# State-space stages of a four-layer kernel: decay by one spreading product per unit, difference and rectifier on ScalarE, causal limit as a 0/1 product on VectorE

## The chip, the cores and the metric

The kernel runs on one core of one Trainium2 chip. A core has TensorE (matrix products, written to PSUM), VectorE, ScalarE, GpSimd and SyncE, each with its own queue that it works through in order; they wait for each other through semaphores. The metric is the time of one execution on the device in microseconds (us), the median of several runs.

## The reference, cut to what matters

The whole program is a stack of four layers, each a mixer and a feed-forward part, over 16 sequences of 256 tokens with 128 channels. Two of the mixers are state-space stages, and only these are touched. The recurrence of the third layer's mixer, with 16 heads of width 16 and a state of 64:

```python
delta = softplus(dt + delta_param)
a_bar = exp(-delta * abs(dt))
h = a_t[:, :, None, None] * h + x_t[..., None] * b_t[:, :, None, :]
y_t = einsum('bhds,bhs->bhd', h, c_t)
```

The fourth layer's mixer (called mamba in the kernel) is of the same kind, with 4 heads of width 64, one B and C for all heads, and `A_bar = exp(A * dt)`. In both, the decay between step s and a later step t is the exponential of the difference of two cumulative sums of logarithms, `exp(cum[t] - cum[s])`, for t >= s and zero for t < s, and all logarithms are at most zero.

## The kernel before

`ssm_block` (from line 901) builds both stages; `ssm` is the stage with 16 heads, `mamba` the one with 4. The 16 sequences are worked in 8 pairs, the first written out (`pair(0, False)`) and the others in a hardware loop. A pair has a setup and a loop over units.

In the setup TensorE projects the input (lines 1062 to 1069), ScalarE and VectorE take the results, VectorE convolves, and from line 1396 on VectorE makes the cumulative sum `cum` of the logarithms and splits it into three bf16 parts, which lie one under the other in `parts` (96 rows, lines 1411 to 1418).

A unit is one head of one sequence, so there are 32 units in a pair of `ssm` and 8 in a pair of `mamba`. It works on 384 columns: the 256 query steps against the first 128 key steps, and the last 128 query steps against the last 128 key steps. The steps of unit u are:

- `unit(u)` on TensorE (line 1117). In each of two column groups `pick` times `parts` spreads the query side's sum (line 1128), `parts` times `unpick` subtracts the key side's sum (line 1130), and `ident16` times `future` adds a very negative number where the key is later than the query (line 1132). That fills `dbank[u % 2]` and counts `decay_up`. Then, for `ssm` in every unit and for `mamba` once per sequence, come the scores, C against B (lines 1150 and 1151), which count `scores_up`.
- ScalarE, line 1281: one `Exp` of 384 columns from `dbank` into `decay[u % 2]`, which counts `decay_done`.
- VectorE, line 1465: `decay` times scores gives `mixer[u % 2]`, which counts `mixer_done`. For `ssm` the scores are read from PSUM, for `mamba` from a copy that line 1457 makes once per sequence.
- `mix(u)` on TensorE: the products of `mixer` with the inputs (lines 1164 and 1165 for `ssm`, 1170 to 1172 for `mamba`), which count `y_up`.

TensorE's order is written out by hand. It looks one unit ahead:

```python
unit(0)
for u in range(units):
    if u + 1 < units:
        unit(u + 1)
    ...
    mix(u)
```

ScalarE's order in the loop is wait for `decay_up` of u, wait for `mixer_done` of u - 2, `Exp` of u. Between some units the late work of the pair before is put in: on VectorE the norms of the tail after units 1, 4 and 7 (0, 2 and 4 in `mamba`), on TensorE and ScalarE the transposes of the tail in `ssm` after unit 10 (lines 171 and 176), and after half of the units VectorE's `take_gated` (lines 1348 and 1353).

Of the kernel before, what the change touches and what calls it, by code (L numbers as in the profile page):

```python
# [20 lines left out]
P = 128  # L21
TILES = SEQS * SEQ // P
PAIRS = SEQS // 2
PT = 4
# [876 lines left out]
def ssm_block(core, name, tail, heads, mamba):  # L901
# [26 lines left out]
    with ExitStack() as ctx:  # L928
# [7 lines left out]
        ident16, future = sb("ident16", [P, P], BF16), sb("future", [P, P], BF16)  # L936
# [40 lines left out]
        decay_up, decay_done = sem("decay_up"), sem("decay_done")  # L977
        scores_up, scores_taken = sem("scores_up"), sem("scores_taken")
# [4 lines left out]
        loads = 12  # L983
# [19 lines left out]
        @block.sync  # L1003
        def _(sp):
            for to, what in ((wx, "wx"), (wdt, "wdt"), (wbc, "wbc"), (wgate, "wgate"), (wout, "wout"), (taps, "taps"),
                             (cols, "cols"), (head_cols, "head_cols"), (pick, "pick"), (unpick, "unpick"),):
                sp.dma_start(to[:], dram[f"{name}_{what}"]).then_inc(weights_in, 16)
            sp.dma_start(ident16[:], dram["identity16"]).then_inc(weights_in, 16)
            sp.dma_start(future[:], dram["future"]).then_inc(weights_in, 16)
# [32 lines left out]
        def _(pe):  # L1042
# [71 lines left out]
            def pair(i, has_late):  # L1114
# [3 lines left out]
                def unit(u):  # L1118
# [6 lines left out]
                    if not (isinstance(i, int) and u < 2):  # L1125
                        pe.wait_ge(decay_done, n - 1)
                    for col, rows, width in ((0, s[0], SEQ), (SEQ, s[1], P)):
                        pe.matmul(bank[:, col:col + width], pick[:, h, :], parts[:, rows:rows + width],
                                  start=True, stop=False)
                        pe.matmul(bank[:, col:col + width], parts[:, rows:rows + P],  # L1130
                                  unpick[:, h:h + 1].broadcast_to([96, width]), start=False, stop=False)
                        last = pe.matmul(bank[:, col:col + P], ident16[:], future[:], start=False, stop=True)  # L1132
                    last.then_inc(decay_up, 1)
# [48 lines left out]
                for kind, n in first_items[-3:-1]:  # L1182
                    _, side, before = place(i, kind, n)
                    pe.wait_ge(down[side], before + 1)
                unit(0)
# [17 lines left out]
        def _(act):  # L1203
# [9 lines left out]
            def pair(i, has_late):  # L1213
# [57 lines left out]
                for c in range(CH):  # L1271
                    act.wait_ge(conv_ready, i * CH + c + 1)
                    flat = conv[:, c].rearrange("p j t -> p (j t)")
                    act.activation(flat, flat, ACT.Silu).then_inc(x_bent, 1)
                for u in range(units):
                    n = i * units + u
                    act.wait_ge(decay_up, n + 1)
# [3 lines left out]
                    act.activation(decay[:, u % 2, :], dbank[u % 2][:, 0:SPAN], ACT.Exp).then_inc(decay_done, 1)  # L1281
# [42 lines left out]
        def _(dve):  # L1324
# [43 lines left out]
            def pair(i, has_late):  # L1368
# [80 lines left out]
                for u in range(units):  # L1449
                    j, h = divmod(u, heads)  # L1450
                    n = i * units + u
                    if not mamba:
                        dve.wait_ge(scores_up, n + 1)
                        scored = gbank[u % 2][:, 0:SPAN]
                    elif h == 0:
                        dve.wait_ge(scores_up, i * 2 + j + 1)
                        dve.tensor_copy(scores[:], gbank[0][:, 0:SPAN]).then_inc(scores_taken, 1)
                        dve.drain()
# [7 lines left out]
                    ins.then_inc(mixer_done, 1)  # L1466
                    if not mamba:
                        dve.drain()
                        dve.sem_inc(scores_taken, 1)
                    if u == heads - 1:  # L1470
                        take_gated(i, 0)
# [1841 lines left out]
def arrange(inputs):  # L3313
# [52 lines left out]
    out["future"] = np.where(t[:, None] <= t[None, :], 0.0, -BIG).astype(bf16)  # L3366
# [96 lines left out]
```

## Time and profile before

| what | value |
|---|---|
| median of 3 runs | 5105.25 us (5102.89 to 5107.88) |
| the profiled execution, its own time | 5086.59 us |
| its span, from first to last instruction | 5084.6 us |
| mean granted clock of TensorE over the span | 0.863 of 2.4 GHz |
| busy share: TensorE, VectorE, ScalarE, GpSimd | 77%, 51%, 44%, 21% |
| the unit loops of `ssm`, first to last start of line 1281 | 2725.7 to 3513.0 us |
| the unit loops of `mamba`, the same | 4081.8 to 4447.5 us |

The profile is of one execution. Busy shares are averages over all the stages, which have different limits, so the two stages have to be read by themselves: in the timeline each row has a start, a length, the engine, the line of the kernel and, in brackets, how long the engine was idle before it and what ended that. The two stages take some 790 and 370 us of the span.

### The profile page before, as it was taken

How to read it: one execution, taken by the hardware profiler on the slowest of the kernel's cores; microseconds unless marked ns; L12 is line 12 of the kernel's file. 1: busy time of each engine (PE TensorE's matmuls, PEld its weight loads, DVE VectorE, ACT ScalarE, POOL GpSimd, SP SyncE). 2: the span in 40 equal slices, each digit the busy share in tenths (PEclk: the TensorE clock that was granted, in tenths of full speed). 3: DMA queues.
4: the chain of work that ended last, by engine and by line, in shares of the span. 5: the costliest groups of instructions: out<-in, count | busy, mean ns of one | idle time of the engine just before them, and what ended most of it. 6: DMA issues, size and time to landing. Idle time of an engine off the chain costs nothing. (4 is left out here: it accounts for less than half of the span.)

```text
span 5084.6 us, 65295 instructions
## 1 busy us (share of the span) xinstructions
PE 3893.2 (77%) x19738; PEld 2713.3 (53%) x19800; DVE 2569.9 (51%) x6625; ACT 2231.9 (44%) x4312; POOL 1045.3 (21%) x1066
## 2 busy tenths in 40 slices
PE   3659954999967688878877888987999877720398
PEld 1137722677734455546555667765677555520266
DVE  5858744222234766477864343342222255579544
ACT  3446533333442688778863433342333333300133
POOL 1012211000001666366640000000000000154200
PEclk9879977899976799989998999998999966655599
DMA  1420021000000000000000000000000000000000
GB/s 38 76 51 7 6 75 54 1 0 0 0 20 0 18 1 0 1 18 1 0 1 16 1 0 0 0 0 33 1 0 0 5 1 0 0 1 0 18 0 17
DMA packets 45622, 58.55 MB, mean 12 GB/s; under 512 B 14058, under 2 KB 37836, under 8 KB 44588
## 3 DMA queue, kind: packets, MB, share of 16 engines
q1 hardware_dynamic: 38956, 50.63, 3.6%
q10 hardware_dynamic: 6528, 6.29, 0.8%
q8 instruction: 61, 1.00, 0.1%
q14 instruction: 77, 0.63, 0.0%
HBM read 34.87 MB, written 10.51 MB: 9 GB/s over the span
## 5 line engine op out<-in xcount | busy, mean ns | idle before, releaser
L418 PEld LDWEIGHTS bank<-moe_w,moe_hidden 128*128 128x128 f32 x5376 | 626.6, 192 | 78.6 <-issue 76.4
L418 PE MATMUL bank<-moe_w,moe_hidden 128*128 128x128 f32 x5376 | 630.3, 275 | 0.0
L408 PE MATMUL bank<-normed_t,moe_w 128*128 (+1 forms) x1344 | 613.9, 599 | 11.0 <-ACT moe_hidden L470 7.6
L470 ACT ACTIVATE moe_hidden<-bank,moe_b 128x512 f32<-128x512 f32 x544 | 372.8, 687 | 504.0 <-PE bank L408 502.5
L546 DVE SCALAR_TENSOR_TENSOR branch<-bank,moe_weights,branch 128x128 f32<-128x128 f32 x768 | 216.2, 344 | 708.1 <-PE bank L418 704.1
L90 POOL TENSOR_TENSOR branch_norm_shifted<-branch_norm_moments,eps 128x4 f32<-128x4 f32 x64 | 12.8, 200 | 1914.0 <-DVE branch_norm_moments L83 1914.0
L408 PEld LDWEIGHTS bank<-normed_t,moe_w 128*128 128x128 f32 x1344 | 244.3, 192 | 254.6 <-issue 239.3
L1960 POOL TENSOR_TENSOR local_size<-local_size,local_half_powers 128x8 f32<-128x8 f32 x128 | 257.2, 2009 | 199.7 <-DVE local_size L2026 195.7
L1465 DVE TENSOR_TENSOR ssm_mixer<-ssm_decay,bank 128x384 f32<-128x384 f32 x256 | 141.8, 554 | 300.8 <-PE bank L1151 263.2
L1281 ACT ACTIVATE ssm_decay<-bank 128x384 f32<-128x384 f32 x256 | 124.9, 491 | 327.4 <-PE bank L1132 327.3
L1664 PE MATMUL bank<-local_wqkv,local_shifted 128*128 128x512 f32 x384 | 211.8, 644 | 58.7 <-ACTq L1837 23.9
L843 PE MATMUL bank<-ident,attn_scaled 128*128 128x128 f32 x32 | 8.9, 432 | 250.0 <-DVE attn_scaled L808 250.0
L1848 ACT ACTIVATE local_probs<-bank,local_peak 128x128 f32<-128x128 f32 x512 | 182.1, 379 | 8.5 <-issue 8.4
L1067 PE MATMUL bank<-ssm_in_rows,ssm_wbc 128*128 128x512 f32 x256 | 142.7, 676 | 45.1 <-ACTq L1264 45.1
L1164 PE MATMUL bank<-ssm_mixer,ssm_x_wide 128*128 128x256 f32 x512 | 158.8, 392 | 19.5 <-DVE ssm_mixer L1465 19.5
L1150 PE MATMUL bank<-ssm_c_rows,ssm_b_rows 128*128 128x256 f32 x512 | 173.2, 421 | 0.0
L1952 POOL TENSOR_TENSOR local_turned_part<-local_raw,local_tables 128x512 f32<-128x512 f32 x128 | 165.8, 1295 | 28.0 <-ACT local_raw L1827 26.8
L1689 PE MATMUL bank<-local_k_t,local_q_t 128*128 128x128 f32 x1024 | 139.8, 281 | 23.7 <-ACT local_probs L1848 20.8
L1689 PEld LDWEIGHTS bank<-local_k_t,local_q_t 128*128 128x128 f32 x1024 | 139.4, 198 | 28.0 <-issue 20.8
L1965 POOL TENSOR_TENSOR local_probs<-local_probs,local_total 128x512 f32<-128x512 f32 x128 | 133.2, 1041 | 81.6 <-DVE local_total L2050 81.6
L2045 DVE TENSOR_REDUCE local_peak<-bank 128x4 f32<-128x512 f32 x128 | 88.5, 691 | 114.6 <-PE bank L1689 107.3
L470 ACT ACTIVATE moe_hidden<-bank 128x512 f32<-128x512 f32 x128 | 76.5, 597 | 152.1 <-PE bank L408 152.1
(535 smaller groups left out, 8933.4 us busy)
## 6 DMA issues: line engine op xcount, KB each, us to landing
rwkv_kept<-rwkv_keep SPq DMA_DIRECT2D x8, 768.0 KB, 15.2
moe_w<-in_moe_w_dram SPq DMA_DIRECT2D x2, 2304.0 KB
rwkv_gate<-rwkv_kept SPq DMA_DIRECT2D x8, 512.0 KB, 3.6
moe_w<-in_moe_w_dram SPq DMA_DIRECT2D x2, 2048.0 KB
rwkv_values<-rwkv_sent_v ACTq DMA_DIRECT2D x16, 128.0 KB
normed_t<-rwkv_sent_b SPq DMA_DIRECT2D x16, 128.0 KB
x<-rwkv_sent_w ACTq DMA_DIRECT2D x16, 128.0 KB
rwkv_recv<-rwkv_sent_r SPq DMA_DIRECT2D x16, 128.0 KB
```

The costliest lines, as they stand in the source:

```text
L408: pe.matmul(hbank[n % 4][:], w1[:, e, f * P:(f + 1) * P], source_t[:, bass.ds(i * PN, PN)], start=True, stop=True).then_inc(hidden_up, 1)
L418: last = pe.matmul(obank[e % 2][:, t * P:(t + 1) * P], hid[:, e % 2, f, t * P:(t + 1) * P], w2[:, e, f, :], start=(f == 0), stop=(f == chu ...
L470: act.activation(hid[:, e % 2, f, :], hbank[n % 4][:], ACT.Gelu_apprx_tanh, bias=b1[:, n:n + 1] if bias else 0.0).then_inc(hidden_done, 1)
L546: last = dve.scalar_tensor_tensor(core.branch[:, t, :], obank[e % 2][:, t * P:(t + 1) * P], weights[:, i * PT + t, e - first_routed:e - fi ...
L1067: last = pe.matmul(bank[0:rows, :], wbc[:, n, :], source, start=True, stop=True)
L1150: pe.matmul(gb[:, 0:SEQ], b[:, s[0]:s[0] + P], c[:, s[0]:s[0] + SEQ], start=True, stop=True)
L1164: pe.matmul(ybank[:, c * SEQ:(c + 1) * SEQ], x[0], m[:, 0:SEQ], start=(k == 0), stop=False)
L1664: pe.matmul(bank[:], shifted[:, at, t * P:(t + 1) * P], wqkv[:, part * INNER:(part + 1) * INNER], start=True, stop=True).then_inc(a_up, 1)
L1689: last = pe.matmul(bank[:, w * P:(w + 1) * P], q_t[:, j, c, w, :], keys, start=False, stop=(w == WINDOWS - 1))
L1848: last = act.activation(probs[:, u % 2, w, :], sbank[u % 2][:, w * P:(w + 1) * P], ACT.Exp, bias=peak[:, u % 2, w:w + 1], accum_out=total[ ...
L1952: pool.tensor_tensor(turned_part[:, m % 2, :].rearrange("p (h s d) -> p h s d", s=2, d=HD // 2), rows, sines.broadcast_to([P, HEADS, 2, HD ...
L1960: pool.tensor_tensor(part, part, half_powers[:], ALU.pow).then_inc(scaled, 1)
```

## The change

The spreading product stays alone on TensorE, 256 columns per unit. The key side's sums are made once per pair, as columns (`shifts`, four small products into `dbank[1]` ahead of `unit(0)`, copied by ScalarE with the sign turned). ScalarE then makes, per unit, the difference and a rectifier in two instructions with a bias column (256 and 128 columns) into the new buffer `falls`, and the `Exp` reads `falls` with scale -1. Since the rectifier makes every difference at least zero, the decay is at most 1 where the key is later than the query, and the causal limit is applied as a product with 0 and 1: for `ssm` by a second VectorE instruction per unit, in place on the two diagonal blocks of `mixer`, and for `mamba` in the copy of the scores, which becomes a product. ScalarE's order is new: it makes the falls of unit u + 1 ahead of the `Exp` of unit u. One load per stage replaces two.

```diff
-        loads = 12
+        loads = 11
...
-            sp.dma_start(ident16[:], dram["identity16"]).then_inc(weights_in, 16)
-            sp.dma_start(future[:], dram["future"]).then_inc(weights_in, 16)
+            sp.dma_start(causal[:], dram["causal"]).then_inc(weights_in, 16)
...
                     if not (isinstance(i, int) and u < 2):
-                        pe.wait_ge(decay_done, n - 1)
-                    for col, rows, width in ((0, s[0], SEQ), (SEQ, s[1], P)):
-                        pe.matmul(bank[:, col:col + width], pick[:, h, :], parts[:, rows:rows + width],
-                                  start=True, stop=False)
-                        pe.matmul(bank[:, col:col + width], parts[:, rows:rows + P],
-                                  unpick[:, h:h + 1].broadcast_to([96, width]), start=False, stop=False)
-                        last = pe.matmul(bank[:, col:col + P], ident16[:], future[:], start=False, stop=True)
-                    last.then_inc(decay_up, 1)
+                        pe.wait_ge(fall_done, n - 1)
+                    if u == 1:
+
+                        pe.wait_ge(shifts_taken, i + 1)
+                    pe.matmul(bank[:, 0:SEQ], pick[:, h, :], parts[:, s[0]:s[0] + SEQ], start=True,
+                              stop=True).then_inc(decay_up, 1)
...
+                if not (isinstance(i, int) and i == 0):
+                    pe.wait_ge(fall_done, i * units)
+                for t in range(PT):
+                    last = pe.matmul(dbank[1][:, t * heads:(t + 1) * heads], parts[:, t * P:(t + 1) * P], unpick[:],
+                                     start=True, stop=True)
+                last.then_inc(shifts_up, 1)
                 unit(0)
...
+                act.wait_ge(shifts_up, i + 1)
+                act.activation(shifts[:].rearrange("p t h -> p (t h)"), dbank[1][:, 0:PT * heads], ACT.Identity,
+                               scale=-1.0)
+                act.drain()
+                act.sem_inc(shifts_taken, 1)
+                def fall(u):
+
+                    j, h = divmod(u, heads)
+                    act.wait_ge(decay_up, i * units + u + 1)
+                    act.activation(falls[:, u % 2, 0:SEQ], dbank[u % 2][:, 0:SEQ], ACT.Relu, scale=-1.0,
+                                   bias=shifts[:, 2 * j, h:h + 1])
+                    act.activation(falls[:, u % 2, SEQ:SPAN], dbank[u % 2][:, P:SEQ], ACT.Relu, scale=-1.0,
+                                   bias=shifts[:, 2 * j + 1, h:h + 1]).then_inc(fall_done, 1)
+
+                fall(0)
+                act.drain()
                 for u in range(units):
                     n = i * units + u
-                    act.wait_ge(decay_up, n + 1)
+                    if u + 1 < units:
+                        fall(u + 1)
 
                     if not (isinstance(i, int) and u < 2):
                         act.wait_ge(mixer_done, n - 1)
-                    act.activation(decay[:, u % 2, :], dbank[u % 2][:, 0:SPAN], ACT.Exp).then_inc(decay_done, 1)
+                    act.activation(decay[:, u % 2, :], falls[:, u % 2, :], ACT.Exp, scale=-1.0).then_inc(decay_done, 1)
+                    act.drain()
...
-                        dve.tensor_copy(scores[:], gbank[0][:, 0:SPAN]).then_inc(scores_taken, 1)
+                        dve.tensor_tensor(scores[:], gbank[0][:, 0:SPAN], causal[:].rearrange("p k t -> p (k t)"),
+                                          ALU.mult).then_inc(scores_taken, 1)
...
                     ins = dve.tensor_tensor(mixer[:, u % 2, :], decay[:, u % 2, :], scored, ALU.mult)
-                    ins.then_inc(mixer_done, 1)
                     if not mamba:
                         dve.drain()
                         dve.sem_inc(scores_taken, 1)
+                        on_time = mixer[:, u % 2, :].rearrange("p (k t) -> p k t", t=P)[:, 0::2, :]
+                        ins = dve.tensor_tensor(on_time, on_time, causal[:, 0::2, :], ALU.mult)
+                    ins.then_inc(mixer_done, 1)
```

The buffers `ident16` and `future` go; `causal`, `shifts` and `falls` come.

## Rows read from the trace of the kernel before

**Rows 1.** The page, part 1: busy time and share of TensorE and weight loads

```profile
PE 3893.2 (77%) x19738; PEld 2713.3 (53%) x19800; DVE 2569.9 (51%) x6625; ACT 2231.9 (44%) x4312; POOL 1045.3 (21%) x1066
```

**Rows 2.** The waits from 2931 to 2995 us: who waited for whom, total, times, longest

```profile
ACT ssm_decay L1281 <- PE bank L1132: 40.7, 29, 3.0
PE bank L1164 <- DVE ssm_mixer L1465: 2.5, 3, 1.4
```

**Rows 3.** Timeline of TensorE in a steady stretch of the ssm loop

```profile
2961.15 0.27 PE L1128 MATMUL bank<-ssm_parts,ssm_pick 96*128 96x256 bf16 x1
...
2961.60 0.65 PE L1150 MATMUL bank<-ssm_c_rows,ssm_b_rows 128*128 128x256 f32 x2
...
2962.31 0.60 PE L1164 MATMUL bank<-ssm_mixer,ssm_x_wide 128*128 128x256 f32 x2
...
2962.96 0.27 PE L1128 MATMUL bank<-ssm_parts,ssm_pick 96*128 96x256 bf16 x1
...
2966.58 0.70 PE L1164 MATMUL bank<-ssm_mixer,ssm_x_wide 128*128 128x256 f32 x2 [0.48 <-DVE ssm_mixer L1465]
```

**Rows 4.** Timeline of ScalarE, same stretch; the last row is two instructions back to back

```profile
2961.80 0.49 ACT L1281 ACTIVATE ssm_decay<-bank 128x384 f32<-128x384 f32 x1 [1.32 <-PE bank L1132]
...
2955.59 0.87 ACT L1281 ACTIVATE ssm_decay<-bank 128x384 f32<-128x384 f32 x2
```

**Rows 5.** Timeline of VectorE, same stretch: two mixers behind one another

```profile
2965.97 0.55 DVE L1465 TENSOR_TENSOR ssm_mixer<-ssm_decay,bank 128x384 f32<-128x384 f32 x1 [0.31 <-ACT ssm_decay L1281]
2966.83 0.55 DVE L1465 TENSOR_TENSOR ssm_mixer<-ssm_decay,bank 128x384 f32<-128x384 f32 x1 [0.30 <-issue]
```

**Rows 6.** Groups by line, ScalarE: with a bias column, by width; rectifier; table loads

```profile
L470 ACT ACTIVATE moe_hidden<-bank,moe_b 128x512 f32<-128x512 f32 x544 | 372.8, 687 | 504.0 <-PE bank L408 502.5
L1848 ACT ACTIVATE local_probs<-bank,local_peak 128x128 f32<-128x128 f32 x512 | 182.1, 379 | 8.5 <-issue 8.4
L3157 ACT ACTIVATE rwkv_relu<-bank 128x512 f32<-128x512 f32 x32 | 18.9, 591 | 41.4 <-PE bank L3118 41.3
L1281 ACT ACT_TABLE_LOAD x16 | 20.5, 1283 | 39.7 <-PE bank L1132 39.7
```

**Rows 7.** Groups by line, VectorE: products of 384 and of 512 columns

```profile
L1465 DVE TENSOR_TENSOR ssm_mixer<-ssm_decay,bank 128x384 f32<-128x384 f32 x256 | 141.8, 554 | 300.8 <-PE bank L1151 263.2 <-ACT ssm_decay L1281 24.0 <-issue 12.9
L1353 DVE TENSOR_TENSOR ssm_gated_t<-bank,ssm_gate 128x512 f32<-128x512 f32 x16 | 11.0, 688 | 16.5 <-PE bank L1165 16.3
```

**Rows 8.** Timeline of TensorE: start of an ssm loop at the lower clock, and its end

```profile
2928.80 0.39 PE L1128 MATMUL bank<-ssm_parts,ssm_pick 96*128 96x256 bf16 x1 [0.93 <-DVE ssm_x_wide L1447]
...
2933.25 1.06 PE L1164 MATMUL bank<-ssm_mixer,ssm_x_wide 128*128 128x256 f32 x2
...
2934.53 0.32 PE L1128 MATMUL bank<-ssm_parts,ssm_pick 96*128 96x256 bf16 x1
...
2994.31 0.38 PE L1165 MATMUL bank<-ssm_mixer,ssm_x_wide 128*128 128x128 f32 x2
```

**Rows 9.** Timeline of TensorE in a mamba loop: its start, one mix, its end

```profile
4179.70 0.28 PE L1128 MATMUL bank<-mamba_parts,mamba_pick 96*128 96x256 bf16 x1 [1.32 <-DVE mamba_x_rows L1441]
...
4187.99 0.63 PE L1170 MATMUL bank<-mamba_x_rows,mamba_mixer 128*128 128x64 f32 x2
...
4189.27 0.42 PE L1128 MATMUL bank<-mamba_parts,mamba_pick 96*128 96x256 bf16 x1
...
4202.44 0.63 PE L1172 MATMUL bank<-mamba_x_rows,mamba_mixer 128*128 128x64 f32 x2
```

**Rows 10.** Windows: length, busy us (instructions) of PE, PEld, DVE, ACT, POOL; clock; DMA

```profile
2935.00:2995.00 60.00, 57.20 (x435) 52.03 (x432) 23.45 (x59) 15.80 (x33) 2.42 (x4) 1.00 0.00 0
4130.00:4153.00 23.00, 21.87 (x106) 18.41 (x103) 13.84 (x45) 5.81 (x10) 3.41 (x5) 0.50 0.00 1
780.00:840.00 60.00, 35.92 (x171) 23.04 (x170) 33.20 (x116) 25.19 (x38) 10.28 (x16) 0.87 0.07 24
1620.00:1680.00 60.00, 33.85 (x92) 20.80 (x91) 30.08 (x117) 5.82 (x10) 10.72 (x18) 0.50 0.04 12
```

More of the change, by code:

```diff
@@ L935, in ssm_block @@
         pick, unpick = sb("pick", [96, heads, P], BF16), sb("unpick", [96, heads], BF16)
-        ident16, future = sb("ident16", [P, P], BF16), sb("future", [P, P], BF16)
+        causal, shifts = sb("causal", [P, 3, P]), sb("shifts", [P, PT, heads])
+        falls, fall_done = sb("falls", [P, 2, SPAN]), sem("fall_done")
         padded = sb("padded", [P, CH, 2, SEQ + TAPS - 1])
@@ L977, in ssm_block @@
         decay_up, decay_done = sem("decay_up"), sem("decay_done")
+        shifts_up, shifts_taken = sem("shifts_up"), sem("shifts_taken")
         scores_up, scores_taken = sem("scores_up"), sem("scores_taken")
@@ L3365, in arrange @@
     out["identity16"] = np.eye(P, dtype=bf16)
-    out["future"] = np.where(t[:, None] <= t[None, :], 0.0, -BIG).astype(bf16)
+    on_time = (t[:, None] <= t[None, :]).astype(np.float32)
+    out["causal"] = np.stack([on_time, np.ones((P, P), np.float32), on_time], axis=1)
     w_in, nw = a["L2_attn_W_in"], a["L2_attn_norm_w"]
```

## The prediction

> **What bounds the kernel now.** I read the page first. TensorE is the busiest engine [rows 1], but that is an average over a dozen stages, and the chain that ended last only covers the final stage, so neither tells what a unit of the state-space stages waits for. The waits of one `ssm` loop do [rows 2]: in 29 of 32 units ScalarE stood waiting for the last decay product on TensorE, while TensorE waited for VectorE's mixer only 3 times, 2.5 us in all. So TensorE bounds the loop and the other two follow. The timeline shows it as a steady beat [rows 3]: a unit takes 2962.96 - 2961.15 = 1.81 us, namely six decay products 0.45 us (2961.15 to 2961.60), scores 0.71 us (to 2962.31) and mix 0.65 us (to 2962.96). Exp and mixer take 0.49 and 0.55 us of it [rows 4, 5] and fit beside it only because of the order: the Exp of unit u starts when `unit(u)` is up, and `mix(u)` comes a whole unit later.
>
> **What comes off TensorE.** Of the six products one of 256 columns stays, about 0.11 us at the full clock if the six are shared out by their columns, 256/1024 of 0.45. That is 0.34 us less per unit, and 256 units would give 87 us if TensorE went on setting the beat.
>
> **What is added, and where.** Per unit ScalarE gets two rectifiers with a bias column. Between 379 ns at 128 columns and 687 ns at 512 [rows 6] the line gives 482 ns for 256; with the 0.49 us of Exp that is 0.48 + 0.38 + 0.49 = 1.35 us. Two Exps back to back took 0.87 us where two single ones take 0.98 [rows 4], an overlap of 0.11 us per neighbour; at best the three take 1.14 us. Both ends are open, I take 1.25. The source of Exp moves from PSUM to SBUF; I cost that at nothing, since it is within the ends. VectorE gets in `ssm` a product of 256 columns: 554 ns at 384 and 688 at 512 [rows 7] give 420 ns. Between the two lie a drain and a semaphore; two mixers behind one another, with a drain, a semaphore and three waits between them, are 0.30 us apart [rows 5], so at most 0.3 us and at least nothing; I take 0.2. The fall buffers and the added drain on ScalarE stand behind the Exp and ahead of a wait for TensorE, so they cost nothing as long as ScalarE is idle, which it is.
>
> **What the new order does.** This is the step that decides. ScalarE now issues the falls of u + 1 ahead of the Exp of u. The falls of u + 1 wait for the spreading product of u + 1, and TensorE issues that only behind `mix(u - 1)`. The Exp of u, the mixer of u and `mix(u)` stand behind them. So each unit is a closed ring: mix, product, two falls, Exp, mixer, causal product, mix. Nothing of one unit runs beside another but the scores. Before, the Exp of u + 1 was ready a unit early; that lead is gone. The ring at the full clock:
>
> - mix(u - 1) to the next product 0.65 us [rows 3]; the product to its end 0.27 us [rows 3];
> - each of the three hand-overs between engines 0.06 us, by the one that rows show bare: mixer end 2966.52 [rows 5], mix 2966.58 [rows 3];
> - falls and Exp 1.25 us (1.14 to 1.35);
> - mixer 0.55, gap 0.2, causal product 0.42.
>
> That is 3.52 us, against 1.81. The scores (0.71 us) lie beside the ScalarE part and are hidden with over 1.5 us to spare. The 87 us on TensorE are therefore worth only what shortens the ring, and are included in it.
>
> At the half clock (1.2 GHz) mix takes 2934.53 - 2933.25 = 1.28 us [rows 8] and the product 0.42 us [rows 9], together 0.78 more: 4.30 us. TensorE then works 0.21 + 1.42 + 1.28 = 2.9 us of it.
>
> **Which clock.** Now the `ssm` loop runs at clock 1.00 with TensorE busy 57 of 60 us, while the `mamba` loop, with TensorE busy 22 of 23 us, stays at 0.50 [rows 10]. Stretches with TensorE busy about 60% have both: 35.9 of 60 us at 0.87, and 33.9 of 60 us at 0.50. In the new ring TensorE is idle for about 2 of 3.5 us at the full clock, and for 1.4 of 4.3 at the half. I expect the clock to go between its two levels and take the mean of the rings, 3.91 us. The Trainium skill ("TensorE: Matmul & The Clock Gate", HAM oscillation) says that only a longer idle gap lets the clock fall, which would give the ring at the full clock all through; it is rival 2. The mamba row above, at the half clock with TensorE hardly ever idle, does not agree that this is all there is to it.
>
> **The sum for ssm.** Before, a loop took from 2928.80 to 2994.69, 65.9 us [rows 8], of which 32 x 1.81 = 57.9 are the beat and 8.0 the start and the tail work. After:
>
> - start: key sums, at most four more products and one small ScalarE copy, 0.35 us; unit 0 and the product of unit 1 at the half clock 0.21 + 1.42 + 0.42 = 2.05; falls 0.76, table load 1.28 [rows 6], Exp 0.49; VectorE 1.17; three hand-overs 0.18: 6.3 us to the first mix, where it was 4.45 (2928.80 to 2933.25);
> - 31 rings of 3.91: 121.2 us;
> - tail work: VectorE has now 2.7 us free in each ring, so that most of the old 8.0 us that wasn't start is hidden. I keep 2 us, since TensorE's and ScalarE's share of it stands in the ring;
> - the last mix 1.0 us.
>
> Together 130.5, so 64.6 us more, and 1.4 us (an estimate: three or four 512-column products at twice their time) for a setup that begins at the lower clock: 66 us per pair, 528 us over 8 pairs. With the full clock all through (ring 3.52, last mix 0.65, no slower setup) it is 52.1 us per pair, 417 in all; with the half clock (ring 4.30, last mix 1.28) 78.4 and 627.
>
> **The sum for mamba.** Before, a loop took 4179.70 to 4203.07, 23.4 us [rows 9]. There is no causal product in its ring: mix 1.28 (4187.99 to 4189.27), product 0.42, falls and Exp 1.25, mixer 0.56, three hand-overs 0.18: 3.69 us at the half clock, which that stage has already. Start 5.6 (6.3 without VectorE's gap and causal product), 7 rings 25.8, last mix 1.3, tail 1: 33.7 us, 10.3 us more per pair, 82 us over 8. The masked copy of the scores costs nothing: 384 columns by 554 ns [rows 7] where a copy of as many columns stood.
>
> **Edits with one answer.** The load is one instruction less on SyncE's queue, and it is issued while GpSimd and VectorE clear buffers; nothing, between -1 and 1 us. A table load at every change between rectifier and exponential would be a disaster, 2 x 1.28 x 320 = 821 us, but the kernel has a rectifier (line 3157) in a stage with exponentials and no table load stands at that line [rows 6]; the loads at line 1281 are 16, one per pair and stage.
>
> So 5086.6 + 610 = 5697 by the profiled execution; that one is 0.37% below the median of the runs, so against the median 5105 + 610 = **5715 us**.
>
> **The rivals.**
>
> 1. *The ring at the half clock all through*: 5105 + 627 + 82 = 5814 us. For it: the mamba rows. Against it: in the half-clock ring TensorE works 2.9 us without a pause.
> 2. *The ring at the full clock all through*: 5105 + 417 + 82 = 5604 us. For it: the 0.87 row; against it: more than half of the ring is a gap.
> 3. *No ring, faster than before.* If the falls of u + 1 and the Exp of u ended before `mix(u)` is due, TensorE would still set the beat, 1.47 us in `ssm`. Its price is -87 us, and in mamba six products of 1.05 us become one of 0.21, up to -54 us, less some 25 us for starts: 4990 us. It decides at the point where product to mix takes less than product and scores on TensorE, 0.82 us; my terms give 2.87. Only if ScalarE did not work in order could that be.
> 4. *A table load at each change of function*: about 6530 us; a row speaks against it.
>
> **How the numbers follow.** The ring with the clock going between its levels 0.45, rival 1 0.22, rival 2 0.26, rival 3 0.03, rival 4 0.02, and 0.02 for what I have not seen. The open terms, 0.1 us each way in ScalarE and about as much in the VectorE gap, are 304 rings (31 x 8 and 7 x 8) x 0.15 = 45 us around each case. The range reaches from rival 2 less 45, rounded down, to rival 1 and 60 over it: 5555 to 5875. About 0.2% is what a measurement of this kernel can tell from no change; all cases but rival 3 are slower by far more.
>
> **What would show it right or wrong.** In the changed kernel ScalarE's falls should start every 3.4 to 4.3 us in `ssm`, with the Exp right behind the second fall and the idle time ahead of the first fall ended by the product at the `pick` line; TensorE's mix should now wait for the causal product in nearly every unit, more than 1 us each time, where it waited 3 times in 32. No table load should stand at the falls but at most one per pair. The granted clock in the loops tells which of forecast and rivals 1 and 2 it was. It is wrong if ScalarE's Exp of u is seen ahead of the product of u + 1, or if ScalarE takes more than 1.35 or less than 1.1 us from the first fall to the end of Exp.

## The result, and the profile after

The changed kernel took **5572.93 us** (median of 4 runs, 5568.17 to 5575.03) against 5104.07 us for the kernel before in the same session (4 runs): a ratio of 1.0918, interval 1.0900 to 1.0937, so 469 us slower. The forecast was 5715 us in a range of 5555 to 5875. The two profiled executions have spans of 5572.0 and 5084.6 us, 487 us apart; the sums below are made between these two.

The page of the changed kernel, parts 1, 2 and 5 (busy time with its share; PEld is TensorE's loading of weights; PEclk is the granted clock in tenths over 40 equal slices of the span; in part 5 busy time, mean ns of one, then the idle time of the engine before the group and what ended it):

```profile
PE 3901.5 (70%) x18202; PEld 2654.6 (48%) x18264; DVE 2674.9 (48%) x6881; ACT 2450.6 (44%) x4968; POOL 1044.2 (19%) x1066
...
PEclk9889887999868998999789889888799966665599
...
L1163 PE MATMUL bank<-ssm_mixer,ssm_x_wide 128*128 128x256 f32 x512 | 201.4, 479 | 420.6 <-DVE ssm_mixer L1494 419.9
L1489 DVE TENSOR_TENSOR ssm_mixer<-ssm_decay,bank 128x384 f32<-128x384 f32 x256 | 141.7, 554 | 593.3 <-ACT ssm_decay L1303 565.6
...
L1289 ACT ACTIVATE ssm_falls<-bank,ssm_shifts 128x256 f32<-128x256 f32 x256 | 121.5, 475 | 578.9 <-PE bank L1131 578.6
```

TensorE issues 1536 matmuls fewer than in [rows 1] and is busy as long as before; its share fell from 77% to 70%. The three groups name each other: the mix (line 1163) stood 420 us for the causal product, VectorE's mixer 566 us for the Exp, ScalarE's first fall 579 us for the spreading product. Each engine waits for the one before it in the ring. The waits of one `ssm` loop, from 2890 to 3016 us, say the same by count (total us, times, longest):

```profile
ACT ssm_falls L1289 <- PE bank L1131: 70.7, 29, 3.5
DVE ssm_mixer L1489 <- ACT ssm_decay L1303: 67.7, 28, 4.9
PEld bank L1163 <- DVE ssm_mixer L1494: 59.7, 32, 3.2
PE bank L1163 <- DVE ssm_mixer L1494: 52.9, 31, 3.0
```

Where TensorE waited for VectorE 3 times in a loop [rows 2], it now does 31 times in 32 units, 1.7 us each. One turn of the steady beat, first TensorE:

```profile
2984.85 0.27 PE L1131 MATMUL bank<-ssm_parts,ssm_pick 96*128 96x256 bf16 x1
2984.96 0.59 PE L1149 MATMUL bank<-ssm_c_rows,ssm_b_rows 128*128 128x256 f32 x2
...
2987.54 0.70 PE L1163 MATMUL bank<-ssm_mixer,ssm_x_wide 128*128 128x256 f32 x2 [1.77 <-DVE ssm_mixer L1494]
...
2988.30 0.27 PE L1131 MATMUL bank<-ssm_parts,ssm_pick 96*128 96x256 bf16 x1
```

then ScalarE in the same turn (two falls, Exp):

```profile
2985.16 0.47 ACT L1289 ACTIVATE ssm_falls<-bank,ssm_shifts 128x256 f32<-128x256 f32 x1 [2.31 <-PE bank L1131]
2985.53 0.36 ACT L1291 ACTIVATE ssm_falls<-bank,ssm_shifts 128x128 f32<-128x128 f32 x1
2985.78 0.52 ACT L1303 ACTIVATE ssm_decay<-ssm_falls 128x384 f32<-128x384 f32 x1
```

and VectorE (mixer, causal product):

```profile
2986.39 0.55 DVE L1489 TENSOR_TENSOR ssm_mixer<-ssm_decay,bank 128x384 f32<-128x384 f32 x1 [2.35 <-ACT ssm_decay L1303]
2987.06 0.43 DVE L1494 TENSOR_TENSOR ssm_mixer<-ssm_mixer,ssm_causal 128x256 f32<-128x256 f32 x1
```

Read across the three fences, no row but the scores overlaps another engine's. Product to product is 2988.30 - 2984.85 = 3.45 us, where [rows 3] had 1.81, and each of the three engines is idle for 1.77 to 2.35 us of it. The same turn at the half clock, from another loop (TensorE):

```profile
3101.48 1.22 PE L1163 MATMUL bank<-ssm_mixer,ssm_x_wide 128*128 128x256 f32 x2 [1.15 <-DVE ssm_mixer L1494]
...
3102.92 0.42 PE L1131 MATMUL bank<-ssm_parts,ssm_pick 96*128 96x256 bf16 x1
...
3105.77 0.48 PE L1163 MATMUL bank<-ssm_mixer,ssm_x_wide 128*128 128x256 f32 x1 [1.14 <-DVE ssm_mixer L1494]
```

4.29 us. By the distances between the starts of Exp, 30 turns in each of the 8 loops are whole (240): 183 of them are 3.46 us and 40 are 4.3, as in the two turns shown at the two clocks. 14 more hold tail work, the 6th (4.67) and the 11th (4.36) of every loop but the first, and 3 lie between. The 31st distance is 0.6 us. The 4.3 us turns stand at the start of a loop (1st to 4th), behind the 6th, and now and then up to the 15th; from the 16th on every turn is 3.46 us. The 6th turn of a loop, on TensorE, is where the clock falls:

```profile
3066.11 0.70 PE L1163 MATMUL bank<-ssm_mixer,ssm_x_wide 128*128 128x256 f32 x2 [3.00 <-DVE ssm_mixer L1494]
...
3066.98 1.06 PE L1149 MATMUL bank<-ssm_c_rows,ssm_b_rows 128*128 128x256 f32 x2
```

TensorE waits 3.00 us instead of 1.77, still does the mix at the full clock, and the scores right behind it at the half (1.06 us for 0.59). Last, ScalarE at the start of that loop:

```profile
3041.10 0.22 ACT L1281 ACTIVATE ssm_shifts<-bank 128x64 f32<-128x64 f32 x1 [1.96 <-PE bank L1187]
...
3043.58 1.28 ACT L1303 ACT_TABLE_LOAD   x1
```

One table load, at the first Exp of the loop; none stands at the falls.

**Where the 487 us lie**, by the starts of Exp:

| stretch | before, us | after, us | more |
|---|---|---|---|
| start to first Exp of `ssm` | 2725.7 | 2734.7 | 9.1 |
| `ssm`, first to last Exp inside the 8 loops | 486.2 | 883.1 | 396.9 |
| `ssm`, last Exp of a loop to first of the next, 7 times | 301.1 | 326.6 | 25.4 |
| last Exp of `ssm` to first of `mamba` | 568.8 | 581.2 | 12.4 |
| `mamba`, inside the 8 loops | 149.9 | 182.4 | 32.5 |
| `mamba`, between them, 7 times | 215.9 | 226.3 | 10.5 |
| last Exp of `mamba` to the end | 637.1 | 637.6 | 0.5 |

The clock of the stretches from first to last Exp is a row of the windows (length, busy us of PE, PEld, DVE, ACT, POOL, granted clock, DMA). Before, `ssm` and `mamba`:

```profile
2726.00:3513.00 787.00, 699.97 (x4177) 542.72 (x4176) 308.75 (x669) 308.13 (x545) 29.02 (x49) 0.94 0.00 0
4082.00:4448.00 366.00, 286.72 (x1256) 211.24 (x1255) 206.17 (x570) 124.52 (x198) 34.80 (x63) 0.64 0.00 0
```

After:

```profile
2735.00:3944.00 1209.00, 725.32 (x2924) 510.86 (x2924) 414.40 (x922) 478.32 (x1059) 28.74 (x49) 0.87 0.00 0
4526.00:4934.00 408.00, 254.94 (x960) 177.06 (x960) 201.80 (x568) 167.51 (x328) 33.70 (x63) 0.62 0.00 0
```

### The profile page after: what moved, and what is told of

Same layout as the page of the kernel before. It is cut to its first block and busy times, and to the rows that moved or that the text cites. A ratio compares the mean times of both kernels' runs of the same rounds, so it can differ in the third digit from the quotient of the medians.

```text
span 5572.0 us, 63225 instructions
## 1 busy us (share of the span) xinstructions
PE 3901.5 (70%) x18202; PEld 2654.6 (48%) x18264; DVE 2674.9 (48%) x6881; ACT 2450.6 (44%) x4968; POOL 1044.2 (19%) x1066
## 5 line engine op out<-in xcount | busy, mean ns | idle before, releaser
L1163 PE MATMUL bank<-ssm_mixer,ssm_x_wide 128*128 128x256 f32 x512 | 201.4, 479 | 420.6 <-DVE ssm_mixer L1494 419.9
L1289 ACT ACTIVATE ssm_falls<-bank,ssm_shifts 128x256 f32<-128x256 f32 x256 | 121.5, 475 | 578.9 <-PE bank L1131 578.6
L1163 PEld LDWEIGHTS bank<-ssm_mixer,ssm_x_wide 128*128 128x128 f32 x512 | 84.8, 208 | 475.0 <-DVE ssm_mixer L1494 475.0
```

The lines of the kernel that those rows point to most:

```text
L1163: pe.matmul(ybank[:, c * SEQ:(c + 1) * SEQ], x[0], m[:, 0:SEQ], start=(k == 0), stop=False)
```

## The experiments

Two questions were open. Is it the order that closes the ring (theory A), or the added work (theory B)? And what holds the clock up in it? All edits but that of e6 are made to the changed kernel. The kernel before took 5097.41, 5095.73 and 5097.65 us in the three sessions (5104.07 beside the changed kernel); each ratio is against its own. e1, e2, e4 and e5 were made in the first, e3, e6 and e7 in the second, e8 and e9 in the third. So a difference between two kernels of different sessions can hold up to 8 us that are not theirs.

### e1: the Exp of u ahead of the falls of u + 1

```diff
 for u in range(units):
-    if u + 1 < units:
-        fall(u + 1)
...
     act.activation(decay[:, u % 2, :], falls[:, u % 2, :], ACT.Exp, scale=-1.0).then_inc(decay_done, 1)
+    if u + 1 < units:
+        fall(u + 1)
```

> The change with one thing moved: ScalarE makes the falls of unit u + 1 behind the Exp of u, as the kernel before had its order. All added work stays. Theory A (the order closes the ring: the Exp of u waits for the product of u + 1): the lead of one unit is back, so two units share one round of product, falls, Exp, mixer, causal product and mix, which the trace of the changed kernel puts at 3.46 us with another 0.1 to 0.2 for the drain that now lies between falls and Exp. A unit then takes 1.75 to 1.9 us in ssm, and the kernel 5060 to 5180 us, about what it took before the change. Theory B (the added work on ScalarE and VectorE costs the time, in whatever order): units stay above 3 us and the kernel above 5450 us.

5150.52 us, ratio 1.0098 (1.0068 to 1.0129). That is in theory A's range. Swapping two calls, with every instruction kept, takes away 422 of the 469 us. The stretch of `ssm` is 827 us instead of 1209:

```profile
2732.00:3559.00 827.00, 632.26 (x2931) 461.18 (x2930) 414.11 (x924) 500.52 (x1063) 28.85 (x49) 0.93 0.00 0
```

It isn't as fast as before, and the timeline says why. The distances between Exps alternate, 1.4 and 2.2 us, mean 1.82. Followed through the engines, TensorE:

```profile
2995.74 0.70 PE L1163 MATMUL bank<-ssm_mixer,ssm_x_wide 128*128 128x256 f32 x2 [0.66 <-DVE ssm_mixer L1494]
...
2996.49 0.27 PE L1131 MATMUL bank<-ssm_parts,ssm_pick 96*128 96x256 bf16 x1
...
2999.38 0.70 PE L1163 MATMUL bank<-ssm_mixer,ssm_x_wide 128*128 128x256 f32 x2 [0.54 <-DVE ssm_mixer L1494]
```

ScalarE:

```profile
2996.80 0.47 ACT L1289 ACTIVATE ssm_falls<-bank,ssm_shifts 128x256 f32<-128x256 f32 x1 [1.01 <-PE bank L1131]
...
2997.62 0.52 ACT L1301 ACTIVATE ssm_decay<-ssm_falls 128x384 f32<-128x384 f32 x1
```

and VectorE:

```profile
2998.23 0.56 DVE L1489 TENSOR_TENSOR ssm_mixer<-ssm_decay,bank 128x384 f32<-128x384 f32 x1 [1.25 <-ACT ssm_decay L1301]
2998.90 0.43 DVE L1494 TENSOR_TENSOR ssm_mixer<-ssm_mixer,ssm_causal 128x256 f32<-128x256 f32 x1
```

The ring is still there, 2999.38 - 2995.74 = 3.64 us from mix to mix, 0.18 us longer than in the changed kernel. But the product behind mix(u - 1) now feeds mix(u + 1), not mix(u): two units travel in it, 3.64 / 2 = 1.82 us each. That is a rule which the other kernels test: **the beat is the ring divided by the units in it, or TensorE's own work if that is longer.**

### e2 and e3: the spreading product further ahead on TensorE

ScalarE keeps the order of the change. In e2 the product of u + 2 is issued ahead of the scores of u + 1; in e3 the product of u + 3 behind them, so ahead of mix(u). Both wait on the same `fall_done` counts. `spread(u)` is the product of unit u with its waits, taken out of `unit(u)`; the two edits in one, shortened:

```diff
+spread(0)
+spread(1)
 unit(0)
+spread(2)                  # e3 only
 for u in range(units):
+    spread(u + 2)          # e2 only
     if u + 1 < units:
         unit(u + 1)
+    spread(u + 3)          # e3 only
...
     mix(u)
```

> The change with its ScalarE order kept, but TensorE issues the spreading product of unit u + 2 ahead of the scores of u + 1, so one unit earlier than now; the banks are the same two. Theory A: the product of u + 1 is up before mix(u - 1), so the round of 3.46 us is shared by two units, 1.73 us each; TensorE's own work is 1.47 us and is not the bound. About 31 x 8 x (1.81 - 1.73) = 20 us in ssm under the time before, starts some 15 us over it, mamba some 30 us under it: 5040 to 5120 us. Theory B: above 5450 us.

> As e2, but TensorE issues the spreading product of u + 3 behind the scores of u + 1, two units earlier than the change does. Theory A: three units now share the round of 3.46 us, 1.15 us each, which is under TensorE's own 1.47 us and under ScalarE's 1.2 us or so; so TensorE sets the beat again, 1.47 us at the full clock. Against e2 (two units in 3.45 us) that is 0.25 us less in 240 units, -60 us, and something in mamba: 5030 to 5060 us, faster than the kernel before. Rival D: the drains and the order on ScalarE and VectorE (two instructions there, three here, each behind the other) keep a round of two units whatever TensorE does: 1.7 us per unit, no change against e2.

e2: 5107.82 us, ratio 1.0015 (1.0000 to 1.0030), in theory A's range. The Exps of `ssm` in e2:

```profile
2983.52 0.52 ACT L1312 ACTIVATE ssm_decay<-ssm_falls 128x384 f32<-128x384 f32 x1
...
2984.94 0.52 ACT L1312 ACTIVATE ssm_decay<-ssm_falls 128x384 f32<-128x384 f32 x1
...
2986.98 0.52 ACT L1312 ACTIVATE ssm_decay<-ssm_falls 128x384 f32<-128x384 f32 x1
```

Their distances alternate 1.42 and 2.04 us: the ring of 3.46 with two units in it, 1.73 each.

e3: 5067.15 us, ratio 0.9935 (0.9920 to 0.9950), faster than the kernel before by 29 us, though 7 us over what was expected. Three units share the ring, 1.15 us each, and that is less than TensorE's own work. TensorE in e3:

```profile
2961.63 0.27 PE L1129 MATMUL bank<-ssm_parts,ssm_pick 96*128 96x256 bf16 x1
2961.74 0.60 PE L1169 MATMUL bank<-ssm_mixer,ssm_x_wide 128*128 128x256 f32 x2
...
2962.39 0.60 PE L1155 MATMUL bank<-ssm_c_rows,ssm_b_rows 128*128 128x256 f32 x2
...
2963.05 0.28 PE L1129 MATMUL bank<-ssm_parts,ssm_pick 96*128 96x256 bf16 x1
```

1.42 us from product to product with no idle time noted: TensorE bounds the plain unit again, so rival D falls, 0.39 us below the 1.81 of [rows 3], with all the added instructions of the change in place. Of 256 x 0.39 = 100 us only 25 show in the stretch of `ssm` (787 to 762 us). Inside the loops it is 44 us (486 to 442), since units with tail work take 2.1 to 5.4 us and every loop has its start, and the stretches between the loops are 19 us longer (301 to 320).

```profile
2738.00:3500.00 762.00, 621.32 (x2917) 459.19 (x2916) 413.36 (x922) 477.75 (x1059) 28.30 (x49) 0.90 0.00 0
```

### e4 and e5: the causal product left out, and made twice

e4 leaves out what limits the mixer to earlier steps in `ssm`, so its output isn't the reference's. Each of the two has 2 runs.

```diff
-ins = dve.tensor_tensor(on_time, on_time, causal[:, 0::2, :], ALU.mult)   # e4: left out
...
 ins = dve.tensor_tensor(on_time, on_time, causal[:, 0::2, :], ALU.mult)
+dve.drain()                                                               # e5
+ins = dve.tensor_tensor(on_time, on_time, causal[:, 0::2, :], ALU.mult)
```

> The change without the causal product in ssm (so nothing there limits the mixer to earlier steps). Theory A (every piece of the ring counts in full): the ring of ssm is shorter by the distance from the end of the mixer to the end of the causal product, 0.55 us by the trace (2986.39 + 0.55 to 2987.06 + 0.43), so 2.9 us at the full clock and 3.7 at the half; 240 rings give -132 us, 5440 us. Theory C (the causal product is hidden beside other work): no change, 5573 us.

> The change with the causal product made twice in ssm, the second behind another drain; its factors are 0 and 1, so nothing else changes. It makes TensorE's gap in each ring longer by about 0.5 us. Theory A with the clock holding: the ring is 3.97 us, 240 rings give +125 us, 5698 us. Theory A with a clock that falls when the gap grows: more than the 47 of 240 rings of the changed kernel run at the half clock, each 0.83 us longer, up to 5860 us. It tells how near the granted clock is to falling, which is the step where forecast and rival 2 parted.

e4: 5430.10 us, ratio 1.0642 (1.0600 to 1.0684), 143 us less than the changed kernel, where theory A had 132; 208 of its 240 turns are 2.91 us, 0.55 less than 3.46, which is the product and the gap ahead of it (0.43 + 0.12). Theory C falls: whatever stands in the ring is paid in full, once a turn.

e5: 5826.11 us, ratio 1.1418 (1.1375 to 1.1461), 253 us more, where 240 turns of 0.54 us longer give 130. Of its turns 86 are 3.96 us (nearly 3.46 + 0.54) and 124 are 4.79 (nearly 4.29 + 0.54): at least 84 turns went over to the half clock, 84 x 0.83 = 70 us, and the stretches between the loops are 29 us longer. The rest lies in the turns with tail work and wasn't separated. The timeline of TensorE in the first loop shows that this happens in the steady beat, with no unit with tail work near:

```profile
2759.51 0.70 PE L1163 MATMUL bank<-ssm_mixer,ssm_x_wide 128*128 128x256 f32 x2 [1.65 <-DVE ssm_mixer L1496]
...
2763.47 0.70 PE L1163 MATMUL bank<-ssm_mixer,ssm_x_wide 128*128 128x256 f32 x2 [2.27 <-DVE ssm_mixer L1496]
...
2767.43 1.22 PE L1163 MATMUL bank<-ssm_mixer,ssm_x_wide 128*128 128x256 f32 x2 [2.06 <-DVE ssm_mixer L1496]
```

Two mixes come at the full clock (0.70 us), the next at the half (1.22 us), behind waits of 2.3 us at most. The mix in e5, and the windows row of its `ssm` stretch:

```profile
L1163 PE MATMUL bank<-ssm_mixer,ssm_x_wide 128*128 128x256 f32 x512 | 260.7, 604 | 466.5 <-DVE ssm_mixer L1496 466.2
```

```profile
2743.00:4189.00 1446.00, 908.49 (x2924) 640.76 (x2924) 522.12 (x1176) 478.43 (x1059) 28.81 (x49) 0.69 0.00 0
```

The same mix took 479 ns on average in the changed kernel and 604 here; the clock of the stretch went from 0.87 to 0.69 although TensorE's instructions are the same 2924. So the clock did not hold, as the second case of the expectation has it.

### e6: the causal product alone, put into the kernel before

The buffer `causal` and its load come with it and aren't shown.

```diff
...
 ins = dve.tensor_tensor(mixer[:, u % 2, :], decay[:, u % 2, :], scored, ALU.mult)
-ins.then_inc(mixer_done, 1)
 if not mamba:
     dve.drain()
     dve.sem_inc(scores_taken, 1)
+    on_time = mixer[:, u % 2, :].rearrange("p (k t) -> p k t", t=P)[:, 0::2, :]
+    ins = dve.tensor_tensor(on_time, on_time, causal[:, 0::2, :], ALU.mult)
+ins.then_inc(mixer_done, 1)
```

> The kernel before with one part of the change alone: the causal product on VectorE in ssm, behind the mixer, with the drain, and its load. Theory A: before, the mixer ended 1.05 us ahead of its mix (2963.07 against 2964.12), and the causal product with its gap takes 0.55 us, so it is hidden in a steady unit; only units behind tail work, some 3 of 32 in which TensorE waited for the mixer anyway, are longer by 0.55: 3 x 8 x 0.55 = 13 us, so 0 to +15 us. Theory B (added VectorE work costs in whatever order): 256 x 0.55 = +140 us.

5136.79 us, ratio 1.0076 (1.0063 to 1.0089): 41 us, where 141 us (256 x 0.55) would be the price in a closed ring and 0 to 15 were expected. Theory B falls. The plain units keep their 1.81 us (170 of them, 184 before); the cost is in the others. The mix in the kernel before and in e6:

```profile
L1164 PE MATMUL bank<-ssm_mixer,ssm_x_wide 128*128 128x256 f32 x512 | 158.8, 392 | 19.5 <-DVE ssm_mixer L1465 19.5
```

```profile
L1166 PE MATMUL bank<-ssm_mixer,ssm_x_wide 128*128 128x256 f32 x512 | 161.5, 398 | 42.7 <-DVE ssm_mixer L1472 42.5
```

TensorE's waits for VectorE grow by 23 us, of 35 us that the `ssm` stretch is longer (787.3 to 822.3). They stand where it waited already, 3 or 4 times a loop, and behind the last unit. One stands behind the transposes of a unit with tail work; first TensorE, then VectorE, then the wait of ScalarE in that loop:

```profile
2969.71 0.70 PE L1166 MATMUL bank<-ssm_mixer,ssm_x_wide 128*128 128x256 f32 x2 [1.21 <-DVE ssm_mixer L1472]
```

```profile
2968.56 0.56 DVE L1467 TENSOR_TENSOR ssm_mixer<-ssm_decay,bank 128x384 f32<-128x384 f32 x1 [2.98 <-PE bank L1153]
2969.23 0.43 DVE L1472 TENSOR_TENSOR ssm_mixer<-ssm_mixer,ssm_causal 128x256 f32<-128x256 f32 x1
```

```profile
ACT normed_t L176 <- PE bank L171: 3.2, 1, 3.2
```

ScalarE waited 3.2 us for these transposes and copied their result before its next Exp, so VectorE got its decay late, and now it makes the causal product on top. At the same place the kernel before has a wait of 0.66 us, 0.55 less. So VectorE's slack of an average unit hides the product, and that of a unit with tail work doesn't. The other part is TensorE's own time: its busy time in the stretch is 715 us where it was 700 for the same products, at a granted clock of 0.92 where it was 0.94:

```profile
2730.00:3553.00 823.00, 714.66 (x4183) 553.35 (x4181) 413.58 (x924) 307.16 (x545) 30.21 (x49) 0.92 0.00 0
```

### e7: the scores made twice

The changed kernel with TensorE's two scores products of each `ssm` unit issued a second time ahead of the first. They lie beside ScalarE's part of the ring.

```diff
+if not mamba:
+    pe.matmul(gb[:, 0:SEQ], b[:, s[0]:s[0] + P], c[:, s[0]:s[0] + SEQ], start=True, stop=True)
+    pe.matmul(gb[:, SEQ:SPAN], b[:, s[1]:s[1] + P], c[:, s[1]:s[1] + P], start=True, stop=True)
 pe.matmul(gb[:, 0:SEQ], b[:, s[0]:s[0] + P], c[:, s[0]:s[0] + SEQ], start=True, stop=True)
```

> The change with the scores products of ssm made twice into the same place: 0.71 us more on TensorE per unit at the full clock, 1.43 at the half. Both lie beside ScalarE and VectorE, where TensorE has 2.0 us free at the full clock and 1.3 at the half, so at the full clock they cost nothing. Theory E (the granted clock falls for want of TensorE activity): the 47 of 240 rings at the half clock go to the full one, 0.83 us each, -39 us, and the mean clock in the ssm loops rises from 0.87 to 0.95 or more: 5534 us. Theory F (the clock follows the gaps alone, in which nothing changes by more than 0.7 us): rings at the half clock stay, each a little longer, 5573 to 5590 us.

5549.02 us, ratio 1.0888 (1.0872 to 1.0904): by medians 24 us faster than the changed kernel, by the ratios 15, with a thousand matmuls more, and between the two theories (5534, and 5573 or more). The intervals of the ratios touch, so the stretch has to decide; it is 29 us shorter (1209 to 1180), the rest of the program 5 us longer:

```profile
2740.00:3920.00 1180.00, 827.91 (x3938) 622.26 (x3939) 414.34 (x922) 476.98 (x1059) 29.94 (x49) 0.95 0.00 0
```

The granted clock is 0.95 instead of 0.87. 212 turns are 3.46 us, the 14 with tail work stay at 4.67 and 4.36, and of the 40 at 4.3 none is left; 8 at 4.0 to 4.1, most of them right behind the 6th turn, are what remains. Against 40 x 0.83 = 33 us that is the 29 found. This and e5 move the clock from both sides with the ring's other work untouched. Neither moves one thing alone: the second scores fill part of the wait ahead of the mix, which is 1.11 us where it was 1.77, and e5's turn has both a longer wait and the same TensorE work in more time.

### e8 and e9: is the product free in an open ring, and do both remedies add up?

e8 is e3 without the causal product (the edit of e4, so its output isn't the reference's either); e9 is e3 with ScalarE's order of e1.

> The kernel with the spreading product two units ahead (e3, 5067 us, units 1.42 us apart by the starts of Exp), without its causal product in ssm, so that its output there is not the reference's. Question: is the causal product free once nothing closes a ring, or does it cost what it cost in the kernel before (e6, +41 us)? Theory C (TensorE sets the beat in e3, VectorE has 1.0 us of work in a beat of 1.42): the product is hidden in the plain units and costs only at the starts of the loops and in units with tail work, where VectorE is late; 5045 to 5065 us, the units of Exp still 1.4 us apart. Rival D (VectorE's chain mixer, causal product, mix already ends last in e3's plain units): the beat falls by 0.1 us or more, 256 x 0.1 = 26 us and the tail units on top; under 5040 us.

> Both remedies together: the spreading product two units ahead as in e3 (5067 us), and ScalarE's falls of u + 1 behind the Exp of u as in e1. If the ring is opened by either, and TensorE sets the beat in e3, the order on ScalarE no longer matters: within 10 us of e3, 5057 to 5077. If ScalarE's Exp of u is still late behind the falls of u + 1 in e3 (their product waiting for a bank), putting it first gains: 5040 to 5056 us. If the falls now come too late and give their bank back too late (the product of u + 3 waits for the falls of u + 1), it loses: 5080 to 5110 us.

e8: 5042.68 us (6 runs, 5022.18 to 5056.38), ratio 0.9886 (0.9864 to 0.9908), 24 us under e3 and between the two figures expected. The plain beat is the same 1.42 us, so rival D falls; the stretch of `ssm` is still 25 us shorter (762 to 737). With e6 that makes a second kernel in which the product costs nothing in a plain unit and 25 to 35 us over the stage.

e9: 5051.28 us (4 runs, 5049.15 to 5064.90), ratio 0.9908 (0.9894 to 0.9922), 16 us under e3 by medians, more than the 10 that would have meant "no matter". It isn't clear of noise: the two intervals just overlap, and e3's six runs reach from 5044.92 to 5079.08. In its profile the `ssm` stretch is 748 us and the `mamba` stretch 346 (762 and 350 in e3), with the plain beat at the same 1.42 us. The difference is behind units with tail work: there the Exps of e9 catch up at 1.22 us each where those of e3 follow at 1.29 to 1.54. That fits with an Exp that no longer waits for a later unit's product. By its median it is the fastest kernel here that computes the whole thing: 46 us under the kernel before, 522 under the change as it was made.

```profile
2740.00:3489.00 749.00, 625.73 (x2922) 462.90 (x2922) 413.36 (x923) 480.66 (x1063) 28.83 (x49) 0.90 0.00 0
```

## Why the prediction was right, and where its sizes were off

**The new order closes a ring: right, and shown.** Each mark that the forecast asked for is in the profile: falls every 3.46 to 4.3 us with the Exp right behind them, idle time ahead of them ended by the product, the mix waiting for the causal product 31 times in a loop by 1.7 us, one table load per loop. e1 shows that it is the order: same instructions, 422 us less. e2, with ScalarE's order kept, opens it from TensorE's side. e6 shows that it isn't the added VectorE work, e3 that it isn't anything else the change brings, since all of it is still there. Rival 3 (no ring) is refuted for this order, and rival 4 (table loads) outright.

**The terms of the ring.** Forecast 3.52, measured 3.45 us, from the three fences of one turn:

| term | forecast | measured |
|---|---|---|
| mix to the next product | 0.65 | 0.76 (2987.54 to 2988.30) |
| product | 0.27 | 0.27 |
| three hand-overs | 0.18 | 0.04 + 0.09 + 0.05 = 0.18 |
| falls and Exp | 1.25 | 1.14 (2985.16 to 2986.30) |
| mixer | 0.55 | 0.55 |
| gap | 0.2 | 0.12 |
| causal product | 0.42 | 0.43 |

The mix was taken from a beat in which TensorE didn't wait. After a wait it is 0.1 us longer, and a row on show said so: 0.60 us in the run, 0.70 at 2966.58 behind a wait [rows 3]. ScalarE took the lower end, since the overlap of [rows 4] holds for all three. The Trainium skill ("ScalarE: Activation LUTs", What ACT_TABLE_LOAD costs) gives 93 ns for that overlap, 0.833 ns per column, and a fixed part of 280 ns with a column operand and 186 without; an estimate by its figures has 1.20 us for the three, and this trace has 1.14. That the sum is off by only 0.07 us is partly luck: 0.11 too little in the mix cancels 0.11 too much on ScalarE. At the half clock it was 4.30 against 4.29.

**Rings per loop: one too many.** The forecast had 31 in `ssm` and 7 in `mamba`. The last unit has no falls of a next unit ahead of its Exp, which follows the one before at 0.6 us. That is 8 x (3.91 - 0.6) = 26 us in `ssm` and 8 x (3.69 - 0.6) = 25 us in `mamba`. In `mamba` the 48 turns left, in 182.4 - 8 x 0.6 us, are 3.70 us each where 3.69 was the forecast, but that is luck: the plain turn is 3.58 us, and the two of a loop that hold tail work (4.07 and 3.89), which the forecast had outside its rings, bring the mean up.

**Which clock: the right case, the wrong mean.** The step "I expect the clock to go between its two levels and take the mean of the rings, 3.91 us" is the largest miss. It does go between them, but only 40 turns are at the half clock. Without the 14 that hold tail work the mean is 3.46 + 40 x 0.83 / 240 = 3.60 us, so 240 x 0.31 = 74 us too many. Half and half was a choice between ends, not a reading, and the time came out nearest to rival 2 (5604 us). Rival 2 is still not what happened: its ring is in about five turns of six, and e7 gets nearly all of the sixth back. Its nearness is partly luck, too: it has the same surplus rings, 8 x (3.52 - 0.6) = 23 us and `mamba`'s 25, about as much as the half-clock turns (33 us) and the stages outside (17 us, below) added. Rival 1 is refuted for `ssm`.

The Trainium skill ("TensorE: Matmul & The Clock Gate", HAM oscillation) ties the fall to a longer idle gap; that nothing else lets the clock fall is the prediction's word. In the changed kernel the trace agrees at one place, the 3.00 us wait of the 6th turn. But the length of one wait doesn't decide. Behind the 11th turn, TensorE waits 2.25 us in seven loops, and the clock falls in three of them and holds in four. e7 has a wait of 2.55 us ahead of the first mix of its last six loops and keeps the full clock behind it (the changed kernel has 2.58 to 2.67 us there, and at least one turn at the half clock at the start of each of these loops), and a shorter one, 2.33 us, in the 6th turn of seven loops, behind which it falls every time; it is back after one turn where the changed kernel needs two and more. In the first loop of e5 it falls in a beat whose waits are 2.3 us at most. e7 speaks for what TensorE does around the wait, since that work is its only edit; the same 2.25 us wait with two outcomes says that this isn't all either. What sets the clock in such a beat stays open.

**Starts and tails: right in `ssm`, too high in `mamba`.** Beside the turns the forecast had 5.6 us per `ssm` loop, 45 us over 8: 130.5 - 121.2 after, less 65.9 - 60.8 before (60.8 is the table's 486.2 by 8 loops), and 1.4 for a slower setup. Measured, from the last Exp to the next first one it is 25.4 / 7 = 3.6 us, 29 over 8, and the tail work in the turns is 7 x (4.67 - 3.46) + 7 x (4.36 - 3.46) = 15 us: 44. In `mamba` it had 3.2 us per loop, 26 in all, and measured 10.5 / 7 = 1.5, 12 in all: 14 too many. Some 5 of these are rightly the ring's, 48 x 0.11 us, by the plain turn of 3.58.

**The balance.** 610 - 26 - 74 - 1 - 25 - 14 = 470 us for the two stages. In the table the four rows of the loops make 465, with 7 stretches between them and not 8; the eighth, at the start of a stage, is in the rows ahead (3.6 and 1.5). The other 17 us of the 487 lie ahead of `ssm`, between the stages and behind them, in stages that the change doesn't touch; the experiments have the first Exp of `ssm` anywhere from 2730.2 to 2742.8 us. Why it moves was not tried.

**TensorE's 87 us** were forecast to be worth nothing in a closed ring. In the changed kernel nothing of them is to be seen. Once the ring is open they show in the beat of 1.42 us, and in part in the time: e3 and e9 are 29 and 46 us faster than the kernel before.

## What to carry to other kernels

When engines hand a unit around, write down for each engine which unit's instruction stands ahead of which, follow one unit from an instruction back to the next one of its kind, and count how many units are in that ring: the beat is the ring over the units, or the busiest engine's own work, whichever is longer. Here one, two and three units in a ring of 3.5 us gave 3.46, 1.73 to 1.82 and 1.42 us, by nothing but the order of issue; the last is TensorE's own work. A step that is moved to a follower with much idle time is free in the plain units only; price it in the units with extra work as well.

## What the hardware showed that was not expected

- Work added to TensorE made the kernel faster: a thousand matmuls more in the shadow of the ring, clock 0.87 to 0.95 in the stretch, 29 us less. In the other direction, 0.54 us more of VectorE in the turn lowered it to 0.69 and cost 123 us beyond its own time, of which 70 are in the turns that went over to the half clock.
- A wait of 2.55 us didn't let the clock fall and one of 2.33 us in the same run did (e7).
- One wait that is longer by 1.2 us, in a unit with tail work, is followed by two or more turns at the half clock: the 7th and the 8th in 7 of 8 loops. The first loop has no such wait there, and no such turns.
- Behind a wait two mixes took 0.70 us where they took 0.60 in a run at the same clock.
